# Cross-attention scores from one fp32 copy of q in 32-row groups

## The reference, cut to what matters

```python
xn = layernorm(x)                                    # no gain, no bias
q, k, v = xn @ Wq + bq, ctx @ Wk + bk, ctx @ Wv + bv # 16 heads of q, one shared head of k and v
scores = einsum('bhqd,bkd->bhqk', q, k) / sqrt(16)
scores = where(mask == 0, -1e9, scores)
x = x + (softmax(scores) @ v) @ Wo + bo
# then x = x + feed_forward(layernorm(x)): a 3-tap mix along the tokens, 9 expert paths, of which the
# arg max of a small gate is taken per token, and a layernorm with gain and bias
```

## Time and profile before

| | |
|---|---|
| times of three runs | 394.74, 399.10, 399.69 us; median 399.1 |
| the profiled execution | 399.22 us, of which the trace's span is 397.1 us; 2.1 us lie around it |
| PE busy | 346.2 us, 87% of the span |
| DVE busy | 298.8 us, 75% |
| POOL busy | 196.6 us, 50% |
| ACT busy | 182.3 us, 46% |
| mean granted clock of TensorE | 0.968 of full speed |

### The profile page before, as it was taken

How to read it: one execution, slowest core, us unless ns; L and a number is a source line. 1 busy time by engine, 2 the same in 40 slices (tenths; PEclk the granted TensorE clock), 3 DMA queues, 4 the chain that set the end, 5 groups by cost and what they waited for, 6 DMA issues and landing times.

```text
span 397.1 us, 7274 instructions
## 1 busy us (share of the span) xinstructions
PE 346.2 (87%) x2636; PEld 279.6 (70%) x2636; DVE 298.8 (75%) x647; ACT 182.3 (46%) x271; POOL 196.6 (50%) x235
## 2 busy tenths in 40 slices
PE   1866984984999999999899999999899999889990
PEld 0745774764877987788577976797588877866890
DVE  3667298498579764789899836889888795699867
ACT  1442725632655366435745374436651455146400
POOL 2640103334206449843939179726944397239234
PEclk9995997999899999999999999999999999999997
DMA  7333452301130004201140105010300110001003
GB/s 209 99 128 95 87 122 72 74 2 26 25 98 1 18 11 111 67 2 26 63 109 0 26 0 172 0 26 0 107 2 0 29 53 2 2 0 54 1 2 106
DMA packets 24004, 20.10 MB, mean 51 GB/s; under 512 B 10593, under 2 KB 20650, under 8 KB 23978
## 3 DMA queue, kind: packets, MB, share of 16 engines
q1 hardware_dynamic: 22338, 19.18, 18.1%
q10 hardware_dynamic: 1640, 0.57, 0.6%
HBM read 9.26 MB, written 4.19 MB: 34 GB/s over the span
## 4 chain that ended last, share of the span: by engine, by line
PE 56%; DVE 21%; issue 13%; ACT 3%; POOL 3%; DMA 2%; SPq 0%; DVEq 0%; POOLq 0%; ACTq 0%
PE ps L429 8%; PE ps L569 5%; PE ps L434 4%; PE ps L652 4%; PE ps L634 4%; PE ps L657 4%; PE ps L653 4%; PE ps L503 3%; PE ps L529 3%; PE ps L530 3%; PE ps L559 3%; PE ps L532 2%; DVE mx L1094 2%; DVE st L1038 2%; PE ps L544 2%
## 5 line engine op out<-in xcount | busy, mean ns | idle before, releaser
L1399 POOL TENSOR_TENSOR rs<-ve,halfneg 128x4 f32<-128x4 f32 x24 | 25.3, 1052 | 154.1 <-DVE ve L1054 154.0
L1087 DVE SCALAR_TENSOR_TENSOR ql<-ps,bqs,qh 64x512 fp32r<-64x512 f32 x32 | 24.0, 750 | 30.7 <-ACT qh L807 30.3
L820 ACT ACTIVATE e<-ps 128x1024 f32<-128x1024 f32 x32 | 32.9, 1027 | 19.8 <-PE ps L532 19.8
L1094 DVE TENSOR_REDUCE mx<-ps 128x16 f32<-128x1024 f32 x32 | 37.9, 1214 | 2.5 <-PE ps L503 2.5
L652 PE MATMUL ps<-w2h,hmh 128*128 128x256 f32 (+1 forms) x140 | 35.1, 286 | 0.0
L653 PE MATMUL ps<-w2l,hmh 128*128 128x256 f32 (+1 forms) x140 | 34.4, 281 | 0.0
L1444 POOL TENSOR_TENSOR hml<-hs,hmh 128x512 fp32r<-128x512 f32 x24 | 30.1, 1271 | 6.5 <-ACT hmh L874 6.5
L569 PE MATMUL ps<-wo,osb 128*128 128x256 f32 x128 | 30.8, 386 | 1.7 <-DVE osb L1112 1.7
L429 PE MATMUL ps<-xmh,w1h 128*128 128x512 f32 x80 | 26.9, 417 | 5.9 <-ACT xmh L845 5.4
L1433 POOL TENSOR_TENSOR y<-xh2f,gms 128x256 f32<-128x256 f32 x28 | 23.6, 872 | 13.4 <-DVE xh2f L1063 13.4
L864 ACT ACTIVATE hs<-ps,b1s 128x512 f32<-128x512 f32 x28 | 19.3, 688 | 23.4 <-PE ps L434 23.1
(11 more groups left out here) (156 smaller groups left out, 884.8 us busy)
## 6 DMA issues: line engine op xcount, KB each, us to landing
xin<-in_x SPq DMA_DIRECT2D x8, 512.0 KB, 3.9
qh<-mT SPq DMA_DIRECT2D x16, 256.0 KB, 3.8
out<-y SPq DMA_DIRECT2D x7, 512.0 KB, 3.1
ql<-thT SPq DMA_DIRECT2D x16, 128.0 KB, 2.4
min_<-in_mask_Bx1xSxS_ik SPq DMA_DIRECT2D x8, 128.0 KB, 3.8
cst<-in_constants SPq DMA_DIRECT2D x1, 768.0 KB, 6.9
cst<-in_constants SPq DMA_DIRECT2D x1, 660.5 KB, 6.0
hs<-in_L_ffn_W SPq DMA_DIRECT2D x2, 288.0 KB
```

The costliest lines, as they stand in the source:

```text
L820: nc.scalar.activation(e[:, 2 * i:2 * i + 2, :], ps[:, bank:bank + 2, :], ACT.Exp).then_inc(s_e, 1)
L1094: v.tensor_reduce(mx[:, k, :].rearrange("p (a h) -> p a h", a=2), ps[:, bank:bank + 2, :].rearrange("p a (h s) -> p a h s", s=SK), AX.X, A ...
```

## The change

q is kept once, as fp32: ACT copies it out of PSUM in two full-width instructions (`q_copy`, 128 x 512 each, where `q_hi` had four of 64 x 512), and DVE rounds it in two (`q_round`, in place of the four of `q_lo`) for the scores for the maxima alone. The transposed scores are fp32 products over the 32 rows of two heads (`kst[quarter(g)]` with `q[quarter(g), t]`): four of them, in the four 32-row groups of the array and in banks 2 to 5, are one half of the step (t = 0 or 1). To each bank two short bfloat16 products are added: an identity with the transposed mask over 64 rows, and a selector of -1 with the transposed maxima over 32 rows. Mask and maxima come out of their transposes already repeated in all row groups, so the DMAs `place_mask` and `place_maxima` are gone, and SyncE issues the feed-forward weights and the next inputs without waiting behind them. The scores for the maxima are, for 128 tokens, two mask products of 512 columns and four fp32r products of 256 columns over 64 rows each. `scores_transposed` is called twice a step, for t = 0 before `wq` and for t = 1 behind it. GpSimd's eight key instructions a row become two.

```diff
-            def scores_transposed(b, j, front):
-                if front:
-                    pe.wait_ge(s_mT, at(b, NJ, j + 2))
-                pe.wait_ge(s_ql, at(b, NJ, j + 1))
-                pe.wait_ge(s_nrow, at(b, 32 * NJ, 32 * (j + 1)))
-                pe.wait_ge(s_mx, at(b, NJ * NT, (j + 1) * NT))
-                for p in range(NPAIR):
-                    q, c = p // 2, slice((p % 2) * P, (p % 2 + 1) * P)
-                    bank = 2 + p % 4
-                    if p >= 4 and p % 2 == 0:
-                        pe.wait_ge(s_e, at(b, NJ * 4, j * 4 + p // 2 - 1))
-                    nc.tensor.matmul(ps[:, bank, :], kmh[:, q % 2, c], qh[:, q, :], start=True, stop=False)
-                    nc.tensor.matmul(ps[:, bank, :], kml[:, q % 2, c], qh[:, q, :], start=False, stop=False)
-
-                    nc.tensor.matmul(ps[:, bank, :], kms[:, q, c], ql[:, q, :],
+            def scores_transposed(b, j, t, front):
+
+                if t == 0:
+                    if front:
+                        pe.wait_ge(s_mT, at(b, NJ, j + 2))
+                    pe.wait_ge(s_q, at(b, NJ * KD, (j + 1) * KD))
+                    pe.wait_ge(s_km, at(b, 3, 2))
+                    pe.wait_ge(s_mx, at(b, NJ * NT, (j + 1) * NT))
+                for g in range(4):
+                    if t and g % 2 == 0:
+                        pe.wait_ge(s_e, at(b, NJ * 4, j * 4 + g // 2 + 1))
+                    nc.tensor.matmul(ps[:, 2 + g, :], kst[quarter(g), :], q[quarter(g), t, :], start=True, stop=False)
+                for g in (0, 2, 1, 3):
+                    r = half_rows(g // 2)
+                    nc.tensor.matmul(ps[:, 2 + g, :], mask_ident[r, 0:P], mT[r, j, :], start=False, stop=False)
+                if t == 0:
+                    pe.wait_ge(s_nT, at(b, NJ, j + 1))
+                for g in range(4):
+                    nc.tensor.matmul(ps[:, 2 + g, :], max_rows[quarter(g), t * P:(t + 1) * P], nmT[quarter(g), :],
                                      start=False, stop=True).then_inc(s_st, 1)
...
-                for q in range(NQ):
-                    bank = banks[k % 2] + q // 2
-                    mm = nc.tensor.matmul(ps[:, bank, (q % 2) * 256:(q % 2 + 1) * 256],
-                                          qh[:, q, k * P:(k + 1) * P], kmh[:, q % 2, :],
-                                          start=True, stop=True)
+                for a in range(2):
+                    r = half_rows(a)
+                    nc.tensor.matmul(ps[:, bank + a, :], mT[r, j, ks], mask_ident[r, :], start=True, stop=False)
+                for m in range(KD):
+                    for a in range(2):
+                        r = half_rows(a)
+                        mm = nc.tensor.matmul(ps[:, bank + a, m * 256:(m + 1) * 256], qr[r, m, ks], kmx[r, :],
+                                              start=False, stop=(m == KD - 1))
                 mm.then_inc(s_sn, 1)
...
                 if n:
-                    scores_transposed(*n, front)
+                    scores_transposed(*n, 0, front)
                 if front:
                     wq(*front, fb)
+                if n:
+                    scores_transposed(*n, 1, front)
...
-                    for par in range(2):
-                        r, _ = halves(par)
-                        a = nc.scalar.activation(qh[r, 2 * m + par, :], ps[r, bank + m, :], ACT.Identity, bias=bqs[r, m:m + 1])
-                a.then_inc(s_qh, 1)
+                    nc.scalar.activation(q[:, m, :], ps[:, bank + m, :], ACT.Identity, bias=bqs[:, m:m + 1]).then_inc(s_q, 1)
...
-            def q_lo(b, j, bank):
-                dve.wait_ge(s_qh, at(b, NJ, j + 1))
+            def q_round(b, j):
                 for m in range(KD):
-                    for par in range(2):
-                        r, _ = halves(par)
-                        a = v.scalar_tensor_tensor(out=ql[r, 2 * m + par, :], in0=ps[r, bank + m, :], scalar=bqs[r, m:m + 1],
-                                                   in1=qh[r, 2 * m + par, :].bitcast(F32), op0=ALU.add, op1=ALU.subtract)
-                a.then_inc(s_ql, 1)
+                    dve.wait_ge(s_q, at(b, NJ * KD, j * KD + m + 1))
+                    a = v.tensor_copy(qr[:, m, :], q[:, m, :])
+                a.then_inc(s_qr, 1)
```

More of the change, by code:

```diff
@@ L42 @@
 KD = D // P
-NQ = 4
 NPAIR = H // 2
@@ L58, with as_bf16, max_column @@
 C_N = C_IO + NPATH
+def as_bf16(ones, word=0x3F80):
+    return np.where(ones, word, 0).astype(np.uint16).view(np.float32)
+def max_column(h):
+    return h % 8 // 4 * 8 + h // 8 * 4 + h % 4
 def constants():
@@ L231, in layer_program, with quarter, half_rows @@
         mr = mask.rearrange("b o (j k p) s -> p (b o) j k s", p=P, k=NT)
-        def halves(par):
-            return (slice(0, 64), slice(64, 128)) if par == 0 else (slice(64, 128), slice(0, 64))
+        def quarter(g):
+            return slice(32 * g, 32 * g + 32)
+        def half_rows(a):
+            return slice(64 * a, 64 * a + 64)
         def banks_for_max(n, f):
@@ L310, in hi @@
             def hi(self, m, r):
-                return qh[0:r, m, :] if m < 4 else xTh[0:r, 0, :]
+                return lhh[0:r, m, :] if m < 4 else xTh[0:r, 0, :]
             def lo(self, m, r):
-                return ql[0:r, m, :] if m < 4 else xTl[0:r, 0, :]
+                return lhl[0:r, m, :] if m < 4 else xTl[0:r, 0, :]
             def x(self, k):
@@ L337, in _ @@
             load(cst[:, C_D4:C_E], consts[:, C_D4:C_E], s_rows)
-            def twice(rows):
-                return rows.rearrange("p (o t) -> p o t", o=1).broadcast_to([rows.shape[0], 2, CH])
-            def place_mask(b, j):
-                sp.wait_ge(s_st, at(b, NJ * NPAIR, j * NPAIR))
-                sp.wait_ge(s_mT, at(b, NJ, j + 1))
-                for par in range(2):
-                    _, mrow = halves(par)
-                    sp.dma_start(qh[mrow, par::2, :].bitcast(F32), twice(mT[mrow, :])).then_inc(s_mrow, 16)
-            def place_maxima(b, j):
-                sp.wait_ge(s_nT, at(b, NJ, j + 1))
-                for par in range(2):
-                    r0 = halves(par)[1].start
-                    sp.dma_start(ql[r0:r0 + 32, par::2, :].bitcast(F32), twice(nmT)).then_inc(s_nrow, 16)
             def next_inputs(b, j):
@@ L371, in row @@
                 for j in range(NJ):
-                    front = (r, 1) if j == 0 else (r + 1, 0)
-                    if more and not feed_forward:
-                        next_inputs(r, j)
-                    if j == 0 or more:
-                        place_mask(*front)
-                    if more and feed_forward:
+                    if more:
                         next_inputs(r, j)
@@ L380, in row @@
                         load_ffn_weights()
-                    if j == 0 or more:
-                        place_maxima(*front)
                     if feed_forward:
@@ L881, in step @@
                 if front:
-                    q_hi(*front, 0 if f else 6)
+                    q_copy(*front, 0 if f else 6)
                 if f:
@@ L1229, in step @@
                     layernorm1_stats(*after)
-                if front and n:
-                    q_lo(*front, 0 if f else 6)
+                if front:
+                    q_round(*front)
                 if f and f[1] == 0:
@@ L1262, in step @@
                         take_max(*front, 3, banks)
-                        negate_max(*front)
+                        split_max(*front)
                 else:
@@ L1267, in step @@
                         take_max(*front, 3, banks)
-                        negate_max(*front)
+                        split_max(*front)
                     if n:
                         x1_stats(*n, 0)
-                if front and not n:
-                    q_lo(*front, 6)
                 if n:
```

155 lines of the change are left out of this document (66 added, 89 removed).

## The result

The changed kernel took **406.9 us** in the median of four runs (401.4 to 407.3) against 399.4 us of the kernel before on the same chip: a ratio of 1.017, 95% interval 1.010 to 1.024. It is slower, by about as much as one measurement can tell from no change. Medians here are over all runs of a kernel, while ratios and their intervals leave out the runs that took over 1.5% more than that kernel's fastest, so the two can differ a little. The forecast was 400 us, "no change", and the range 386 to 411. The profiled execution took 406.49 us with a span of 404.7 us, to be set against 399.2 and 397.1.

A forecast was written before the change was run, and what follows sets the result against it. PE was taken to bound the kernel, meeting ACT's tanh at the gate in every step with a feed-forward part. The terms summed to +0.9 on 399.2 us: forecast 400 us, no change, range 386 to 411 (the forecast's own 395 to 405).

The forecast's parts named there:

- the clock falls: Rival: PE idles 3.2 us before the hidden tiles in steps 3, 5, 7, then half speed loses 1.7 each; 405 us, chance 0.12.
- Steps 4 and 6: Transposed scores and exponentials there: PE saves 1.3 us but waits for ACT about as long; gate S + 13.1, +0.1 a step.
- Steps 5 and 7: Hidden tiles at S + 10.5, gate at S + 16.0, +0.8 us each; in step 5 the wait for osb goes, -0.7.
- Step 3: Half clock until S + 2.1, then later exponentials and xmh put the gate at S + 15.8: +2.0 us.
- Step 8: No q here; the second half waits for two exponentials and ends at S + 6.5 instead of S + 5.7: +0.5 us.
- Steps 1 and 2: PV waits some 1.2 us for the last exponential, the 1.1 us for ql goes: -0.3 each, -0.6 us.
- Before step 1: Step 0: the 1.58 us wait of x's transposes for ql goes: -1.5 us; SyncE's queue counted as hidden, 0.
- Scores for the maxima: Two groups of 64 rows run side by side, 0.7 us with the change of shape as before: 0.
- The bfloat16 transposes: Transposes of the maxima: four end in 0.39 us instead of 0.60, on PE's path in steps 3 to 7: -1.0 us.
- The row groups: Four fp32 products over 32 rows run side by side in 0.87 us; a half of the transposed scores takes 2.2 us.
- Both cases of turns: Rival: row groups take turns; partly, 420 us, chance 0.12; with no overlap at all, 469 us, chance 0.06.
- GpSimd at nothing: GpSimd's six dropped instructions are hidden by other work of steps 1 and 2 and count 0.

The follow-up runs named there:

- experiment 2: Changed kernel with both halves of the transposed scores ahead of q, the order of the kernel before: 414.7 us, ratio 1.039.
- 5: Changed kernel with q cut in two, its first 128 columns ahead of the second half of the transposed scores, the others behind: 400.6 us, ratio 1.006.
- experiment 1: Changed kernel with 12 unused products where PE waits for xmh, in steps 3, 5, 7 and the epilogue: 403.6 us, ratio 1.010.
- 6: Kernel of 5 with the denominators' 64 products moved ahead of the hidden tiles in steps 3, 5 and 7: 403.0 us, ratio 1.012.
- experiment 8: Changed kernel with SyncE's wait of experiment 4, the 12 products of experiment 1, and 18 more at the end of steps 1 and 2: 395.2 us, ratio 0.991.
- experiment 7: Changed kernel with qr rounded from q's PSUM bank plus bias instead of copied from q in SBUF: 407.1 us, ratio 1.022.
- Experiment 4: Changed kernel with SyncE's loads behind the score constants (1.7 MB) held until ScalarE has rounded Wq: 403.0 us, ratio 1.005.

## Why the prediction was right, and where its terms were not

The time lay in the range and "no change" was the call; the sum was 7 us short of 406.9. The rival "the clock falls", with a chance of 0.12, had put 405, and its mechanism is what happened: behind PE's longer idling for `xmh` the clock fell. Not place by place, though. The rival had 3.4 us at half speed in each of steps 3, 5 and 7; the trace has none in step 3, 6.8 in step 5, 3.4 in 7, 6.8 in 8 and 3.4 in the last feed-forward part. The range held partly by luck: steps 1 and 2 saved 1.6 us more than forecast, while the start up to step 1 took 2.0 us more than forecast, steps 5 and 7 together 2.0, and the end 3.6. The prediction argued against the rival that gaps of 2.5 us had left the clock alone. There was one of that length, ahead of the last feed-forward part; it is as long in the changed kernel, and there the clock fell 0.9 us behind it. First before, then changed:

```profile
348.69 0.71 PE L429 MATMUL ps<-xmh,w1h 128*128 128x512 f32 x2 [2.52 <-ACT xmh L845]
```

```profile
355.62 0.70 PE L417 MATMUL ps<-xmh,w1h 128*128 128x512 f32 x2 [2.52 <-ACT xmh L846]
```

So a gap that kept the clock once is no proof that it will again. In experiment 2 it fell behind waits of 1.1 to 1.2 us.

1. *Steps 4 and 6: right.* +0.1 forecast, +0.1 and +0.2 measured; the gate at S + 12.75, forecast S + 13.1. The claim that the gate's place sets the step's length is only half true: in 5 it moved by 0.75 and the step by 0.3.
2. *Steps 5 and 7: mechanism right, size off.* The hidden tiles start at S + 10.1 in step 5 (forecast 10.5), but at half speed, 0.43 us a pass instead of 0.235, so the gate is at S + 17.2 and not 16.0. In step 5 GpSimd's later load adds a second bound that the prediction did not have. Experiments 1 and 6 give 42.5 and 41.2 for step 7 and keep 47 for step 5; experiment 8 splits these 47 into the load's part and the clock's.
3. *Step 3: right.* Gate at S + 15.8, as forecast; +2.1 against +2.0.
4. *Step 8: the term that failed most.* +0.5 was forecast and +4.1 measured to the end. The wait for the exponential was foreseen (the second half starts at S + 3.2, when the first exponential has freed two banks, not at S + 4.4), but not its sequel: half speed through the second half and the first hidden tiles, gate at S + 13.75 instead of the S + 10.3 of before, and once more in the last feed-forward part. With the clock kept (experiments 1 and 7) the term is +0.6.
5. *Steps 1 and 2: mis-sized.* -0.6 forecast, -2.2 measured together; PV's wait for the exponential, 1.1 us, is there as forecast. Part of the difference is the clock, which in step 1 is back at S + 2.1 instead of S + 3.9.
6. *Before step 1: wrong.* -1.5 forecast, +0.5 measured. The waits for `ql` went, but the sentence that SyncE's queue is hidden and "can only gain" was false. A wait ahead of loads is also what keeps them out of the way of more urgent ones. Experiment 4 gives the price, 2.5 us; with its wait the start is 2.0 earlier than before, where -1.5 was forecast.
7. *Scores for the maxima: nearly right.* They overlap, and a group takes 0.56 us (211.26 to 211.82 in step 5) where 0.70 was priced by the earlier trace rows. *The bfloat16 transposes*: four take 0.40, as priced.
8. *The row groups: right.* They run side by side; a half is 2.0 us, priced 2.2. By the page "TensorE: Matmul & The Clock Gate" of the Trainium skill (section on the measured speedup against the span model) the fp32 part would be 1.1 us, an estimate; it is 1.07 up to the first mask product. The second records start 0.53 us behind the first, with no change of shape between them, where a pass of PV took 0.43, so the trace agrees with the factor. The half of 2.4 us estimated from it was too long, since the changes of shape cost less than the earlier trace rows made them: the mask products take 0.54 us up to the first of the maxima, with 0.47 of streaming. The prediction's own 2.2 us came near since the fp32 part cost 0.2 more than its 0.87 and the changes of shape less than their 0.22. Both cases of turns are out, and so is a drain of 0.4 us at each change.
9. *GpSimd at nothing: wrong*, by one microsecond in step 5, through VectorE's moved work (experiment 7).

Open: which gap is followed by half speed differs between kernels and executions. In 7 the wait of step 8 was not, and a gap of step 3 was, both as long as in the changed kernel; one of the four runs of the changed kernel took 401.4 us with a mean clock of 0.956, where the others have 0.937 to 0.941. What decides it no run here shows. Nor is it shown which part of the 3.5 us at the end came back by the added products in experiment 1, since experiment 7 has the same end, 86.6 us, without them.

## What to carry to other kernels

Where an engine is fed by others, price each gap that a change opens on PE twice: once as idle time, and once as the half speed that may follow it, 3.4 or 6.8 us long in these traces behind some gaps and not behind others; then look for work of the same step that fits into it, and only then for products without a use. When a wait is dropped from a queue, ask what stood behind it: loads set free early compete with the ones that the start needs. Test a product's form and its place apart before keeping either: here each alone cost 14 to 15 us, and both together 7.5.

## What the runs showed of the hardware that was not expected

- Short waits can cost the clock. Behind waits of 1.1 us and 0.9 us the granted clock was 0.50 for 3.4 us in step 6 of experiment 2, and behind 1.2 and 0.7 us in step 5 of experiment 1. The same two waits in step 5 of experiment 8 left it at 1.00, and the same 2.52 us ahead of the last feed-forward part cost the changed kernel its clock and the kernel before not.
- 48 products without any use, 11 us of PE's time, made the median some 3 us shorter, within overlapping intervals; with 36 more and SyncE's wait it is 12 us, well clear of them.
- GpSimd's additions of 128 x 256 took 0.73 us each beside VectorE's reads from PSUM and up to 1.19 beside its fp32 work in SBUF, and that work 1.10 instead of 0.75.
- 1.7 MB of loads issued on another queue at about the same time as Wq and bq delayed Wq by 2.6 us and bq, of 1 KB, by 4.7.
